# GpSimd takes a butterfly stage of six weight groups and the remainders of half the turned rows

## The reference

```python
x = x + layernorm(mamba(layernorm(x)))        # selective scan, 1024 channels x 16 states
x = x + layernorm(ffn(layernorm(x)))
# ffn:
x = fwht(x * SU_ug) / SCALE                                   # Hadamard over 512
x = silu(x @ W_gate.T * s_g) * (x @ W_up.T * s_u)             # 2048 wide
x = fwht(x * SU_dp) / SCALE                                   # Hadamard over 2048
x = (x @ W_down.T) * (Wscale_dp * SCALE)
```

## Time and profile before

| what | us |
|---|---|
| median of 3 runs | 2642.16 |
| the profiled run's own time | 2643.02 |
| its span in the profile | 2641.2 |
| TensorE busy | 2573.5 (97%) |
| VectorE busy | 2243.6 (85%) |
| GpSimd busy | 2044.3 (77%) |
| ScalarE busy | 1815.0 (69%) |
| granted TensorE clock, mean | 0.996 of full speed |

### The profile page before, as it was taken

The page is one execution under the profiler, slowest core; times in us unless marked ns, Lnnn a source line. Parts: engine busy times, 40 slices in busy tenths (PEclk is TensorE's granted clock), DMA queues, the critical chain, the costliest instruction groups (busy, mean ns, idle before and its releaser), DMA issues.

```text
span 2641.2 us, 46296 instructions
## 1 busy us (share of the span) xinstructions
PE 2573.5 (97%) x16048; PEld 2185.7 (83%) x16048; DVE 2243.6 (85%) x2573; ACT 1815.0 (69%) x3935; POOL 2044.3 (77%) x1691
## 2 busy tenths in 40 slices
PE   7999989999999999999999999999999999989998
PEld 6566668989888888989888898988888898978888
DVE  6898998899898888899889889989888989889622
ACT  4776777677777777777777767777777777755322
POOL 6776879788787979888797978888797988876322
PEclk9999999999999999999999999999999999999999
DMA  5664246656666666766666665666666566656675
GB/s 182 211 208 167 101 167 215 228 198 240 212 232 219 216 220 205 238 208 229 222 217 226 211 230 198 240 211 231 221 216 220 202 230 211 232 178 225 245 293 192
DMA packets 165209, 564.41 MB, mean 214 GB/s; under 512 B 17264, under 2 KB 19696, under 8 KB 132976
## 3 DMA queue, kind: packets, MB, share of 16 engines
q1 hardware_dynamic: 164976, 561.44, 61.9%
HBM read 527.30 MB, written 34.08 MB: 213 GB/s over the span
## 4 chain that ended last, share of the span: by engine, by line
PE 78%; DVE 10%; ACT 7%; issue 3%; DMA 1%; POOL 1%; SPq 0%; DVEq 0%; ACTq 0%; POOLq 0%
PE pF L726 21%; PE hT L633 14%; PE pM L651 13%; PE pD L742 10%; PE pM L703 8%; DVE h L1205 5%; DVE acc L1218 3%; PE pM L673 3%; PE pD L766 3%; ACT decay L1011 2%; PE decay L726 2%; PE hT L625 1%; PE pF L766 1%; ACT delta L988 1%; ACT delta L983 1%
## 5 line engine op out<-in xcount | busy, mean ns | idle before, releaser
L1205 DVE TENSOR_TENSOR_SCAN h<-decay,dbx 128x512 f32<-128x512 f32 x1024 | 1200.3, 1207 | 72.6 <-ACT decay L1011 44.0
L1389 POOL TENSOR_TENSOR dbx<-u,bb 128x2048 f32<-128x2048 f32 (+1 forms) x272 | 1179.3, 4336 | 37.4 <-DVE h L1205 35.4
L1011 ACT ACTIVATE decay<-delta,a_neg 128x255 f32<-128x255 f32 x2048 | 873.9, 468 | 300.7 <-DVE h L1205 293.6
L1218 DVE SCALAR_TENSOR_TENSOR acc<-hT,bcT,acc 128x1024 f32<-128x1024 f32 x480 | 610.5, 1272 | 138.5 <-PE hT L633 134.7
L726 PE MATMUL pF<-fxT_hi,wug 128*128 128x256 f32 x3712 | 724.6, 288 | 0.0
L726 PEld LDWEIGHTS pF<-fxT_hi,wug 128*128 128x128 f32 x3712 | 595.4, 192 | 0.2
L633 PEld LDWEIGHTS hT<-ident,h 128*128 128x128 f32 x4096 | 473.1, 141 | 140.0 <-issue 90.0
L633 PE MATMUL hT<-ident,h 128*128 128x128 f32 x4096 | 535.8, 274 | 31.7 <-DVE acc L1218 20.5
L726 PE MATMUL pF<-fxT_lo,wug 128*128 128x256 f32 x1856 | 525.3, 283 | 0.0
L651 PE MATMUL pM<-xnT,w_in 128*128 128x256 f32 x2016 | 480.1, 381 | 3.5 <-ACT hid L931 2.1
L651 PEld LDWEIGHTS pM<-xnT,w_in 128*128 128x128 f32 x2016 | 367.3, 191 | 51.0 <-issue 5.0
(11 more groups left out here) (177 smaller groups left out, 2672.3 us busy)
## 6 DMA issues: line engine op xcount, KB each, us to landing
wug<-scratch_ug SPq DMA_DIRECT2D x243, 1024.0 KB, 4.8
wd<-scratch_wd SPq DMA_DIRECT2D x243, 512.0 KB, 4.1
w_in<-in_W_in SPq DMA_DIRECT2D x252, 256.0 KB, 3.0
bb<-scratch_bc SPq DMA_DIRECT2D x128, 256.0 KB, 4.7
xb<-in_hidden_states SPq DMA_DIRECT2D x16, 512.0 KB, 5.0
xr<-in_hidden_states SPq DMA_DIRECT2D x16, 512.0 KB, 5.9
out<-xr SPq DMA_DIRECT2D x15, 512.0 KB, 3.7
kept_ug<-scratch_ug SPq DMA_DIRECT2D x7, 1024.0 KB, 8.1
```

Of the source, the lines that this page charges most:

```text
L1011: e = act.activation(da[q % 2][:, i, 1:], delta[c % 2][:, dt, 1:], ACT.Exp, scale=a_neg[:, dt, n:n + 1])
L1205: dve.tensor_tensor_scan(row(h[n % 2][:, tiles, :]), row(da[q % 2][:, :, :]), row(dbx[n % 2][:, tiles, :]), 0.0, ALU.mult, ALU.add).then_i ...
L1218: dve.scalar_tensor_tensor(acc[c % 2][:, tb, :], hT[:, :], cn, acc[c % 2][:, tb, :], ALU.mult, ALU.add).then_inc(acc_done, 1)
L1389: pool.tensor_tensor(dbx[n % 2][:, tiles, :], u[:, tiles, :], rows, ALU.mult).then_inc(done if restarts(c) else prod_done, 1)
```

## The change

Six of the eight up and gate groups (all but up 0 and up 1) get their first butterfly on GpSimd: `half_sums` adds and subtracts the first and last two tiles of the loaded group, two operations of 128x1024, into another of the three `had_in` tiles. A row of such a group then takes two products instead of four. The groups are put in another order (down 0 to 3 before up 1).

In every group but the first, rows 0 and 2 get their low part in another way. ScalarE writes the unrounded row in fp32 to the place of the low part (a second activation from PSUM), and GpSimd takes the high part from it in place (`had_difference`); VectorE keeps rows 1 and 3. ScalarE now waits for both stores of the set in the first row of a group. A PSUM bank of such a row is free when ScalarE has written it.

`room` changes: 4 steps in slot 0/0, 2 in 0/1 to 0/7, 3 in 0/8 to 0/17, then 2, 1, 1 in turn. A group's half sums stand in the pair that starts four or five slots behind the last step of the group that frees its load buffer (`HAD_ADD`).

```diff
-        GROUPS = ([("up", 0), ("down", 0), ("up", 1)] + [("down", q) for q in range(1, KT)] + [("up", q) for q in range(2, KT)]
-                  + [("gate", q) for q in range(KT)])
+        GROUPS = ([("up", 0)] + [("down", q) for q in range(KT)] + [("up", q) for q in range(1, KT)] + [("gate", q) for q in range(KT)])
...
+        POOL_LO = [o for o in range(KT, NTILE) if o % KT in (0, 2)]
+        DVE_LO = [o for o in range(NTILE) if o not in POOL_LO]
...
-        IN_BUF = dict(zip(UG_GROUPS, (0, 0, 0, 1, 2, 0, 1, 2)))
+        IN_BUF = dict(zip(UG_GROUPS, (0, 0, 1, 0, 2, 1, 0, 2)))
+        WHOLE, SUMMED = UG_GROUPS[:2], UG_GROUPS[2:]
+        SUM_BUF = dict(zip(SUMMED, (2, 1, 0, 2, 1, 0)))
+        LAST_USER = dict(zip(UG_GROUPS, [None, WHOLE[0], LAST_DOWN, WHOLE[1]] + SUMMED))
...
-        steps_of = lambda o: 2 if GROUPS[o // KT][0] == "down" else KT
+        steps_of = lambda o: KT if o // KT in WHOLE else 2
+        FIRST_SUM = 18
...
-                room = (4 if k == 0 or 8 <= k < 16 else 3 if 23 <= k < 28 else 2) if c == 0 else 2
+                at = SLOTS * c + k
+                room = (4 if k == 0 else 3 if k >= 8 else 2) if at < FIRST_SUM else (2, 1, 1)[(at - FIRST_SUM) % 3]
...
-                            HAD_LOAD[at] += UG_GROUPS[3:5] if o // KT == LAST_DOWN else next_in(o // KT) if o // KT in UG_GROUPS else []
+                            for new in [i for i in SUMMED if LAST_USER[i] == o // KT]:
+                                HAD_LOAD[divmod(at + 1, SLOTS)].append(new)
+                                HAD_ADD[divmod((at + 5) // 2 * 2, SLOTS)].append(new)
...
                     if o >= len(had_bank):
-                        pe.wait_ge(had_lo, o - len(had_bank) + 1)
+                        old = o - len(had_bank)
+                        if old in POOL_LO:
+                            pe.wait_ge(had_raw, made(POOL_LO, old))
+                        else:
+                            pe.wait_ge(had_lo, made(DVE_LO, old))
...
+                    if g in SUMMED and r == 0:
+                        pe.wait_ge(had_halved, 2 * (SUMMED.index(g) + 1))
...
+                elif g in SUMMED:
+                    src, last, minus = had_in[SUM_BUF[g]][:, r // 2 * 2 + i, :], i == 1, r % 2 * i
...
                 if r == 0 and split_use(g):
                     act.wait_ge(had_stored[f"{SETS[g]}_hi"], 16 * split_use(g))
+                    act.wait_ge(had_stored[f"{SETS[g]}_lo"], 16 * split_use(g))
                 act.activation(split_row("hi", o), bank_tiles(o), ACT.Copy, scale=had_scale(o)).then_inc(had_hi, 1)
+                if o in POOL_LO:
+                    act.activation(split_row("lo", o).bitcast(F32), bank_tiles(o), ACT.Copy, scale=had_scale(o)).then_inc(had_raw, 1)
...
+            def half_sums(g):
+                src, dst = had_in[IN_BUF[g]], had_in[SUM_BUF[g]]
+                pool.wait_ge(had_loaded[IN_BUF[g]], 16 * (in_use(g) + 1))
+                if SUMMED.index(g):
+                    pool.wait_ge(had_halved, 2 * SUMMED.index(g))
+                pool.tensor_tensor(dst[:, 0:2, :], src[:, 0:2, :], src[:, 2:4, :], ALU.add).then_inc(had_halved, 1)
+                pool.tensor_tensor(dst[:, 2:4, :], src[:, 0:2, :], src[:, 2:4, :], ALU.subtract).then_inc(had_halved, 1)
+
+            def had_difference(o):
+                pool.wait_ge(had_raw, made(POOL_LO, o))
+                pool.tensor_tensor(split_row("lo", o), split_row("lo", o).bitcast(F32), split_row("hi", o).bitcast(F32),
+                                   ALU.subtract).then_inc(had_sub, 1)
...
+                for g in HAD_ADD.get((c, k), ()):
+                    half_sums(g)
+                for at in (SLOTS * c + k - 1, SLOTS * c + k):
+                    for o in HAD_EVAC.get(divmod(at, SLOTS), ()):
+                        if o in POOL_LO:
+                            had_difference(o)
```

More of the change, by code:

```diff
@@ L166, in fused_block @@
         w_out_in = sem("w_out_in"); down_in = [sem("down_in0"), sem("down_in1")]; wscale_in = sem("wscale_in")
[L167 removed]
+        had_loaded = [sem(f"had_loaded{i}") for i in range(len(had_in))]; had_halved = sem("had_halved")
         had_setup = sem("had_setup"); w_first_in = sem("w_first_in"); diag_done = sem("diag_done"); turned_dve = sem("turned_dve"); turned_pool = sem("turned_pool")
[L169 removed]
+        had_mm = sem("had_mm"); had_hi = sem("had_hi"); had_lo = sem("had_lo"); had_raw = sem("had_raw"); had_sub = sem("had_sub")
         had_stored = {name: sem(f"had_stored_{name}") for name in split}
@@ L296, in fused_block, with made, first_of @@
         had_bank = [t[:, :, :].rearrange("p a t -> p (a t)") for t in (pF,)] + [t[:, :] for t in pD]
+        POOL_LO = [o for o in range(KT, NTILE) if o % KT in (0, 2)]
+        DVE_LO = [o for o in range(NTILE) if o not in POOL_LO]
+        def made(table, o):
+            return sum(1 for i in table if i <= o)
+        def first_of(table, g):
+            return next(i for i in table if i // KT == g)
         def split_use(g):
             return SETS[:g].count(SETS[g])
-        IN_BUF = dict(zip(UG_GROUPS, (0, 0, 0, 1, 2, 0, 1, 2)))
+        IN_BUF = dict(zip(UG_GROUPS, (0, 0, 1, 0, 2, 1, 0, 2)))
+        WHOLE, SUMMED = UG_GROUPS[:2], UG_GROUPS[2:]
+        SUM_BUF = dict(zip(SUMMED, (2, 1, 0, 2, 1, 0)))
+        LAST_USER = dict(zip(UG_GROUPS, [None, WHOLE[0], LAST_DOWN, WHOLE[1]] + SUMMED))
         def in_use(g):
             return [IN_BUF[i] for i in UG_GROUPS if i < g].count(IN_BUF[g])
-        def next_in(g):
-            return [i for i in UG_GROUPS if i > g and IN_BUF[i] == IN_BUF[g]][:1]
         def split_row(s, o):
@@ L322, in had_scale @@
             return row_scale[:, KT * GROUPS[g][1] + r:KT * GROUPS[g][1] + r + 1] if GROUPS[g][0] == "down" else su_ug[:, r:r + 1]
-        HAD_PE, HAD_EVAC, HAD_STORE, HAD_LOAD = ({(c, k): [] for c in range(2) for k in range(SLOTS)} for i in range(4))
-        steps_of = lambda o: 2 if GROUPS[o // KT][0] == "down" else KT
+        HAD_PE, HAD_EVAC, HAD_STORE, HAD_LOAD, HAD_ADD = ({(c, k): [] for c in range(2) for k in range(SLOTS)} for i in range(5))
+        steps_of = lambda o: KT if o // KT in WHOLE else 2
+        FIRST_SUM = 18
         HAD_EVAC[0, 0] += [3]
@@ L470, in load_had @@
                 name, q = GROUPS[g]
-                older = [i for i in UG_GROUPS if i < g and IN_BUF[i] == IN_BUF[g]]
-                if older or IN_BUF[g]:
-                    wait_first(sp, had_mm, KT * ((older[-1] if older else LAST_DOWN) + 1), sp_passed)
+                if LAST_USER[g] is not None:
+                    wait_first(sp, had_mm, KT * (LAST_USER[g] + 1), sp_passed)
                 sp.dma_start(had_in[IN_BUF[g]][:, :, :], W[f"W_{name}"].rearrange("(k p) f -> p k f", p=P)[:, :, DM * q:DM * (q + 1)]
@@ L478, in store_had @@
                 name, q = GROUPS[g]
-                for s, (part, done) in enumerate((("hi", had_hi), ("lo", had_lo))):
-                    wait_first(sp, done, KT * (g + 1), sp_passed)
+                for s, part in enumerate(("hi", "lo")):
+                    if part == "hi":
+                        wait_first(sp, had_hi, KT * (g + 1), sp_passed)
+                    else:
+                        wait_first(sp, had_lo, made(DVE_LO, KT * g + KT - 1), sp_passed)
+                        if g:
+                            wait_first(sp, had_sub, made(POOL_LO, KT * g + KT - 1), sp_passed)
                     place = f"{SETS[g]}_{part}"
@@ L1246, in had_low @@
                 dve.wait_ge(had_hi, o + 1)
-                if r == 0 and split_use(g):
+                if o == first_of(DVE_LO, g) and split_use(g):
                     dve.wait_ge(had_stored[f"{SETS[g]}_lo"], 16 * split_use(g))
```

14 lines of the change are left out of this document (8 added, 6 removed).

## The result

The changed kernel takes 2663.63 us (median of 4 runs, 2662.26 to 2663.68), the one before 2640.76 (4 runs, 2639.2 to 2642.7): ratio 1.0084, interval 1.0071 to 1.0098. The difference of the medians is 22.9 us. The sum said +5.7; slower had a chance of 0.39, just under that of no change (0.41), and 2663.6 lies above the range (2632 to 2657).

The account below looks back on a forecast made before the run. It took TensorE as the bound, VectorE and in one stretch GpSimd close behind. Six stretches, 0 + 4.6 - 5.6 - 3.4 + 12.7 - 2.6, gave +5.7 us: 2648.7 profiled, 2647.8 for the median; range 2632 to 2657.

Parts of the forecast that it names:

- The sum: Total over six stretches of slots up to 2/0: the change makes the kernel 5.7 us slower.
- Prices, counts: Whole change: 48 of 160 products leave TensorE (41.3 us), 22 remainders leave VectorE (14.5 us), GpSimd gets 57 us.
- 0/0 to 0/7: Slots 0 to 7 of chunk 0: same TensorE work, which bounds the stretch, so 0 us.
- 0/8 to 0/19: Slots 8 to 19 of chunk 0: GpSimd becomes the bound and the conv silu waits for its taps, +4.6 us.
- 0/20 to 0/31: Slots 20 to 31 of chunk 0: fewer TensorE steps leave VectorE as bound at 47.6 us, -5.6 us.
- 1/0 to 1/3: Slots 0 to 3 of chunk 1: three fewer products in TensorE's chain, and TensorE less late, -3.4 us.
- 1/4 to 1/19: Slots 4 to 19 of chunk 1: GpSimd's longer queue plus ScalarE's wait for the low-part store, +12.7 us.
- the wait 4.5: ScalarE's wait for the low-part store in slots 1/5, 1/11 and 1/17, partly hidden by GpSimd's lateness: 4.5 us.
- the 10% that I had named as a sign against it: Forecast counts as wrong if GpSimd is idle over 10% in slots 4 to 19 of chunk 1.
- 1/20 to 2/0: Slot 20 of chunk 1 to slot 0 of chunk 2: fewer remainders on VectorE, -2.6 us.
- (b): Rival, chance 0.20: GpSimd takes its new work in gaps, TensorE and VectorE decide; faster by 12 us, 2630.
- (c): Rival, chance 0.15: ScalarE's store waits in 1/5, 1/11, 1/17 cost in full, 12 us; slower, +13.2, 2655.4.

Follow-up runs that it names:

- e1: Changed kernel with the evictions (high and raw parts of a row) at the end of ScalarE's slot, in every slot; 2668.22 us, ratio 1.0102.
- e9: Changed kernel with the evictions at the end of ScalarE's slot in nine slots of each chunk only; 2657.77 us, ratio 1.0060.
- e6: Changed kernel with each GpSimd difference issued one pair of slots later; 2653.27 us, ratio 1.0041.
- e5: Changed kernel with the steps from slot 0/18 on as 1, 1, 2 instead of 2, 1, 1; 2658.79 us, ratio 1.0060.
- e2: Changed kernel with row 0 of groups 8 to 11 left to VectorE, ScalarE waiting for low-part stores only before row 2's raw part; 2651.61 us, ratio 1.0040.
- e3: Changed kernel with half sums and new group order kept, but all remainders on VectorE (no differences); 2641.03 us, ratio 0.9998.
- e11: Changed kernel with three repairs: steps 1, 1, 2, differences one pair later, evictions late in nine slots; 2657.21 us, ratio 1.0061.
- e8: e7 with groups 10 and 11 taking whole sums on TensorE, so four groups with half sums; 2628.23 us, ratio 0.9949.
- e7: e3 with steps 1, 1, 2 and the evictions late in nine slots only; 2636.79 us, ratio 0.9980.
- e4: Kernel before, old order and no half sums, with raw parts and GpSimd differences for rows 0 and 2 of groups 1 to 11; 2651.50 us, ratio 1.0039.
- e14: e11 with only row 2's remainder on GpSimd in groups 8 to 11, the store wait ahead of row 2's raw part; 2645.09 us, ratio 1.0014.

## Why the prediction was wrong, step by step

The step that failed is the sum of the first four stretches: it took the busy time of the engine that bounds a stretch, and put what the new operations wait for, and what waits behind them, at 1.1 us in one stretch and at nothing in the others. The runs show 13.8 us more there.

- *Prices, counts*: right. Product records on TensorE 224, remainders on VectorE 26, GpSimd +56.3.
- *0/0 to 0/7, "same TensorE work: 0"*: **failed**, +2.4. The work is the same, but the groups' rows end at other slots. With the evictions late in these slots the stretch is 33.6 (e1, e9). I had looked only at TensorE's sum, not at what stands behind the high part on ScalarE.
- *0/8 to 0/19, "I add 1.1 in all" for GpSimd's waits for ScalarE*: **failed**. The bound (GpSimd) was right; the waits were not. The sum took pair 5's product to start at its old 102.77, with one difference ahead of it. GpSimd was idle 3.1 us (put down to a scan), 4.2 and 4.2 (to the raw part) ahead of the three differences up to pair 5, and its product started 9.5 us later than before; behind it the queue was as summed (51.8 us; 51.9 said). In the stretch itself GpSimd waited 5.2 us for raw parts. There is also a misreading: 152.52 and 303.31 of the earlier trace rows are table loads, which don't wait for the taps (159.32 in the trace after, with the taps still going). The silu itself came 1.3 us behind them and so had 1.3 us more to spare in either chunk than the 1.0 and 3.0 that the sum used. The wait is long because a difference stands in the pair of its own raw part: GpSimd is ahead of the scans there and has to wait until ScalarE gets there. e6, which puts it a pair later, has this stretch at 61.5.
- *0/20 to 0/31, "-5.6", and 1/0 to 1/3, "-3.4"*: **failed**, 9.2 us of the miss together. This is the largest term. The forecast added up busy time per stretch, with VectorE as the bound at 47.6, and left out as a chain a row's last product, its eviction and the next TensorE bank, and GpSimd's differences that wait for it. Moving the evictions alone brings 49.6 and 23.2 (e9). But with the evictions in place the first of the two stretches also falls by other repairs: late differences 50.4 (e6), 1, 1, 2 50.0 (e5), row 0 of group 8 left to VectorE 51.4 (e2), no remainder on GpSimd 50.6 (e3). So it is the order on ScalarE and the remainders together, and no run divides them. The forecast also counted TensorE at 39.7 us of work in 0/20 to 0/31, at the full clock; it was busy 45.1, at a granted clock of 0.94 (e9: 40.9, at 0.97). The diff doesn't show such a change of order: `had_high` is not moved, the products that it waits for are.
- *1/4 to 1/19, "+12.7", of which the wait 4.5*: right in sum (+13.1), nearly in the wait (4.5; the stretch is 3.1 shorter in e5 and 3.7 in e2). GpSimd's queue from the copy ahead of pair 3's product to the last tap takes 76.1 us (249.23 to 325.30), where 72.8 and 3.3 of waiting were said. Right too in the silu, which comes 77.1 us behind pair 3's product instead of 64.7, 12.4 later. The 14.8 us that the page books on the wait are not its price; GpSimd was late anyway, as the forecast had it. GpSimd is idle for 10.8% of the stretch, a little over the 10% that I had named as a sign against it.
- *1/20 to 2/0, "-2.6"*: right.
- *Rivals*: (b), relief, held for no version with all the remainders. (c), slower still, had the sign but put the extra cost on the store's wait; that mechanism was real and near its price, and the extra lay elsewhere. In e11, though, it did decide, with 13 to 16 us for three waits.
- The range was too narrow since each rival varied a term that I had already found. None was "a queue that I had not looked at".

How the 22.9 us divide, as the runs show it: half sums nothing that can be told (e3); remainders beside them 22.6. That it is more their waits than their work is shown for GpSimd by e6: the same operations a pair later, without the waits for raw parts, take 10.4 us less. Single repairs give 4.8 (e5), 5.9 (e9), 10.4 (e6) and 12.0 (e2); they overlap and don't add. Of e8's 12.8 us under e3 the two whole groups bring 8.6 (e7 to e8; 6.7 of it ahead of slot 2/0); the order of evictions and 1, 1, 2 bring 4.2 together and were not separated. Why e4's differences cost 9.8 and those beside half sums 22.6 is not settled: GpSimd's waits for raw parts are as long in e4 (19.6 us), ScalarE's for the store of r_lo are shorter (5.4 us in 3), and the moved rows exist only beside the half sums; no run adds them up one by one.

## What to carry to other kernels

Price a moved operation by the operations queued behind it on every in-order engine that touches it: here 2.4 us for a half sum and 1.3 for a difference were exact, and the miss lay in waits, such as 4.2 us ahead of a product. When work is rescheduled, follow each consumer that was *not* edited, for what it waits now comes at another time. Give a nearly full engine work only in stretches where its sum leaves room. Test repairs together, since two that each help alone (later differences, another order of steps) can make a third wait longer. Read a repair's gain by stretches, for the median alone can put it down to the wrong place (e5). And where a wait can't be avoided, see which queue it stands in: on VectorE the wait for the store cost little, on ScalarE much.

## Not expected of the hardware

The granted clock of TensorE, 1.00 in four of the six stretches of the earlier trace rows, is 0.92 to 0.95 in five of six after. At level 0.5 (1.2 GHz) for the missing share, the stretches of after come to (0.05 x 64.6 + 0.06 x 54.6 + 0.07 x 24.3 + 0.08 x 85.3 + 0.07 x 46.0) / 0.5 = 36.5 us, those of before to 7, and e8 has none. Windows of 2 us around the store's wait in slot 1/5, kernel after:

```profile
258.00:260.00 2.00, 2.00 (x14) 1.50 (x12) 0.10 (x1) 0.00 (x0) 0.78 (x1) 1.00 0.98 264
260.00:262.00 2.00, 0.46 (x2) 0.00 (x0) 0.00 (x0) 1.92 (x4) 0.57 (x1) 1.00 1.05 403
262.00:264.00 2.00, 0.29 (x1) 0.29 (x2) 1.76 (x2) 2.00 (x7) 2.00 (x3) 1.00 0.99 379
264.00:266.00 2.00, 1.03 (x5) 0.58 (x5) 2.00 (x3) 1.81 (x5) 2.00 (x1) 0.76 0.00 1
266.00:268.00 2.00, 2.00 (x9) 1.91 (x9) 2.00 (x3) 0.97 (x3) 1.86 (x3) 0.50 0.00 0
268.00:270.00 2.00, 2.00 (x3) 0.67 (x2) 2.00 (x4) 0.87 (x2) 2.00 (x2) 0.50 0.00 0
```

TensorE stands still from 260.5 to 263.7, and the grant, 1.00 up to 264, falls after it has begun again. Its time line on both sides:

```profile
255.11 1.02 PE L791 MATMUL pD<-had_in,h_plus 128*128 128x512 f32 x2
255.97 2.75 PE L667 MATMUL pM<-xnT,w_in 128*128 128x256 f32 x12
...
263.71 1.13 PE L667 MATMUL pM<-xnT,w_in 128*128 128x256 f32 x4 [3.26 <-ACT hid L959]
...
267.57 3.62 PE L791 MATMUL pD<-had_in,h_plus 128*128 128x512 f32 x4
270.98 3.19 PE L667 MATMUL pM<-xnT,w_in 128*128 128x256 f32 x12
```

A product takes 0.86 us ahead of it (255.11 to 255.97) and 1.7 behind it (267.57 to 270.98 for two). It is not the only such case in this trace. Of the nine falls of the grant in the first 382 us eight come within 1.3 us of the end of a stop of TensorE (stops of 2.6, 3.2, 2.7, 3.8, 3.3, 5.9, 2.8 and 2.7 us); the one at 193.3 us has no stop over 1.2 us in the 8 us before it. So a wait that stops TensorE this long is followed here by some us in which it runs at half rate, and where TensorE then sets the time that is added to the wait. Half of 36.5 less half of 7 is some 14.7 us of TensorE time. It accounts for most of the 17.2 us by which TensorE's busy time fell short of the 41.3 saved, and it is an upper estimate of what the clock costs the change; no run separates it from the waits ahead of it. It isn't in proportion to the loss either: 2 us windows over the same part of e14 add up to 34 us at half rate, and e14 is 18.5 us faster than the change.
